# A two-stage gated layer on one core: the gathers of the rank tiles spread over the steps of the first stage, and the sort, the loads and ScalarE's order in the opening rearranged

## What is computed

```python
# layer 1: of 4 contexts the one that the token's id picks serves as gate, up and down weight
hn = layernorm(x)
e = minimum(ids // 6250, 3)
x = x + tanh(g_xattn) * where_e( (silu(hn @ C[e].T) * (hn @ C[e].T)) @ C[e] )
# layer 2: 16 experts, the best 2 of each token, at most 256 tokens to an expert, and a shared one
xt = layernorm(x)
scores = sqrt(softplus(xt @ gate_w.T)); idx = top_2(scores + gate_b)
y = sum over the two of w * W2[e] @ (silu(xt @ W1[e].T) * (xt @ W3[e].T))   + the shared expert
x = x + tanh(g_ffn) * y
```

## Time and profile before

| | us |
|---|---|
| median of 3 runs | 496.58 |
| lowest, highest | 496.21, 497.57 |
| the profiled execution, its own time | 497.83 |
| its span, first to last instruction | 496.0 |

### The profile page before, as it was taken

How to read it: one execution, slowest core, us unless ns; L and a number is a source line. 1 busy time by engine, 2 the same in 40 slices (tenths; PEclk the granted TensorE clock), 3 DMA queues, 4 the chain that set the end, 5 groups by cost and what they waited for, 6 DMA issues and landing times.

```text
span 496.0 us, 7772 instructions
## 1 busy us (share of the span) xinstructions
PE 464.3 (94%) x2496; PEld 393.5 (79%) x2496; DVE 329.9 (67%) x707; ACT 257.8 (52%) x379; POOL 208.2 (42%) x175
## 2 busy tenths in 40 slices
PE   1889999999999939999999999999999999999993
PEld 1358887888888728888888999999999999888982
DVE  5669998998987534358937976666666666666520
ACT  4744544545553333363253576666666666666531
POOL 0612443664334733541636724444427444332242
PEclk9989999999999969999999999999999999999997
DMA  8626545666545713233629999998969988897545
GB/s 320 233 82 234 170 152 168 233 233 223 169 174 199 246 56 113 86 50 48 85 65 230 211 301 313 234 258 255 261 225 264 280 268 247 259 258 223 107 58 70
DMA packets 29164, 95.02 MB, mean 192 GB/s; under 512 B 4816, under 2 KB 5328, under 8 KB 28624
## 3 DMA queue, kind: packets, MB, share of 16 engines
q0 software_dynamic: 17040, 43.66, 35.4%
q1 hardware_dynamic: 11808, 50.98, 30.8%
q10 hardware_dynamic: 288, 0.01, 0.0%
HBM read 67.50 MB, written 28.70 MB: 194 GB/s over the span
## 4 chain that ended last, share of the span: by engine, by line
PE 84%; DVE 7%; issue 3%; DMA 2%; ACT 1%; another core or an unknown queue 1%; POOLq 0%; POOL 0%; DVEq 0%; ACTq 0%
PE psG L1251 46%; PE psY L1251 28%; PE psT L1256 6%; PE psG L1495 1%; DMA front<-in_x,idx 1%; ACT arena L619 1%; DMA tok_i<-in_ids 1%; DVE stats L908 1%; DVE xh_sb L881 1%; DVE gu L897 1%; DVE arena L886 0%; PE psG L1279 0%; DVE stats L915 0%; DVE big L834 0%
## 5 line engine op out<-in xcount | busy, mean ns | idle before, releaser
L1251 PE MATMUL psY<-arena 128*128 (+2 forms) x372 | 94.4, 401 | 0.0
L1251 PEld LDWEIGHTS psY<-arena 128*128 128x128 f32 (+1 forms) x372 | 67.5, 188 | 13.3
L497 POOL DMA_INDIRECT ht<-out,idx x32 | 34.6, 1081 | 78.2 <-PE psT L1256 62.4
L1251 PE MATMUL psY<-slot,arena 128*128 128x512 f32 (+1 forms) x240 | 61.1, 399 | 0.0
L1026 DVE TENSOR_TENSOR slot<-raw,slot 128x1536 fp32r<-128x1536 f32 x25 | 43.9, 1757 | 23.8 <-ACT slot L615 23.1
L1251 PE MATMUL psG<-arena 128*128 x228 | 58.0, 403 | 0.0
L1026 DVE TENSOR_TENSOR arena<-raw,arena 128x1536 fp32r<-128x1536 f32 x24 | 42.1, 1758 | 22.9 <-ACT arena L615 19.5
L1251 PE MATMUL psG<-arena,slot 128*128 128x512 f32 x216 | 52.6, 399 | 0.0
L1251 PEld LDWEIGHTS psY<-slot,arena 128*128 128x128 f32 (+1 forms) x240 | 43.7, 189 | 9.0 <-ACT xh_sb L659 0.3
L1251 PEld LDWEIGHTS psG<-arena 128*128 128x128 f32 x228 | 42.0, 190 | 10.2 <-issue 1.9
L1251 PEld LDWEIGHTS psG<-arena,slot 128*128 128x128 f32 x216 | 41.1, 193 | 8.5
(11 more groups left out here) (221 smaller groups left out, 809.1 us busy)
## 6 DMA issues: line engine op xcount, KB each, us to landing
raw<-in_w SPq DMA_DIRECT2D x51, 768.0 KB
padded<-xh_sb SPq DMA_DIRECT2D x19, 256.0 KB
raw<-in_ctx_t SPq DMA_DIRECT2D x2, 1024.0 KB, 8.9
ht<-in_ctx_t SPq DMA_DIRECT2D x1, 1024.0 KB, 13.3
xh_sb<-in_ctx_t SPq DMA_DIRECT2D x1, 1024.0 KB, 15.4
out<-log_sb SPq DMA_DIRECT2D x4, 256.0 KB
ht<-out,idx POOLq DMA_INDIRECT x32
xb<-in_x,idx POOLq DMA_INDIRECT x19
```

The costliest lines, as they stand in the source:

```text
L497: pool.indirect_dma_start(ht[:, n, :], None, halves_of_out, slots(e * NA + a, 0)).then_inc(g_here[n], 16)
L1251: ins = pe.matmul(ps, left[a], right[b], start=n == 0 and m == 0, stop=n == total - 1 and m == 2)
```

## The change

1. **Rank gathers.** Tiles 4 to 10 are gathered one in each step from 13 to 19, behind the step's scatter; tile 11 after the loop's last scatter, and 12 to 15 behind it. `row_tile` gives tiles 4 to 7 and 12 to 15 `ht`, tiles 8 and 9 `ys`, tiles 10 and 11 `xa`. The waits for free buffers follow.
2. **Sort.** The triangular matrices, `ones` and `iota` are made bf16 by one activation of ACT (`marks`, over `gu`), and the count totals are bf16 (`tot`), so the prefix matmuls are bf16. `hold` is an instruction that counts on `chain` without a wait. Some instructions go without waits, a multiply and a reduction go ahead of the wait for PE. The one-hot blocks are 16 instructions of 128x128 that come last, and each of the 16 matmuls waits for its own. The list's first column is signalled ahead of its second. The table of contexts by tile (`tile_e`) comes after the list.
3. **Loads.** The fourth context, the bias and the zeros are issued once POOL has issued the first gather (`first_out`).
4. **Contexts.** Context 2 goes by PE and context 1 by DVE. ACT's order: `high_ctx(2)` behind two `take_rest(0, ..)`, `take_rest(2, 0)` and `(2, 1)` behind the first norm, `high_ctx(3)` in step -1.

The core of the diff:

```diff
@@ row_tile
-            return ht[:, j % 4, :] if j % 8 < 4 else front[:, j % 4, :]
+            return ht[:, j % 4, :] if j // TB != 2 else (ys, xa)[j % TB // 2][:, j % 2, :]
@@ sync
-            for e in range(E1):
+            for e in range(E1 - 1):
                 sp.dma_start(ctx_raw(e), ctx_t[e, :, :]).then_inc(ctx_here[e], 16)
+            sp.wait_ge(first_out, 1)
+            sp.dma_start(ctx_raw(E1 - 1), ctx_t[E1 - 1, :, :]).then_inc(ctx_here[E1 - 1], 16)
             sp.dma_start(bias_b[:, :], gate_b).then_inc(in_bias, 16)
@@ gpsimd: rank_gather
-                if j >= 8:
+                if j // TB == 2:
+                    pool.wait_ge(h_ready, 4 if j % TB < 2 else NT)
                     pool.wait_ge(bT_ps, j - 7)
-                elif j >= 4:
-                    pool.wait_ge(hT_ps, NT)
+                elif j >= TB:
+                    pool.wait_ge(bT_ps, j - 3 if j < 2 * TB else j - 7)
@@ gpsimd: the loop over t
-                if t == NT - 1:
-                    for j in range(TB, 2 * TB):
-                        rank_gather(j)
-                if t == NT:
-                    for j in range(2 * TB, 3 * TB):
-                        rank_gather(j)
+                if ROWS0 < t <= ROWS0 + 2 * TB - 1:
+                    rank_gather(t - ROWS0 + TB - 1)
+            rank_gather(3 * TB - 1)
@@ scalar
+            act.wait_ge(in_const, 16)
+            act.activation(marks[:, :], cst[:, 0:4 * P], ACT.Copy).then_inc(digits_ready, 1)
...
             high_ctx(0)
             high_ctx(1)
+            take_rest(0, 0)
+            take_rest(0, 1)
             high_ctx(2)
-            take_rest(0, 0)
-            high_ctx(3)
-            for i in range(1, KD):
-                take_rest(0, i)
-            take_rest(1, 0)
-            take_rest(1, 1)
+            take_rest(0, 2)
+            take_rest(0, 3)
@@ scalar: step
+                if known == -1:
+                    high_ctx(3)
                 if known in (-1, 0):
-                    take_rest(1, known + 3)
+                    take_rest(2, known + 3)
...
+                if known == FIRST:
+                    take_rest(2, 0)
+                    take_rest(2, 1)
@@ vector
             for e in range(1, E1):
-                link(dve.tensor_scalar(S(e), S(0), float(VOCAB1 // E1 * e), None, ALU.is_ge))
-            link(dve.tensor_scalar(S(4), S(1), -1.0, 1.0, ALU.mult, ALU.add))
+                hold(dve.tensor_scalar(S(e), S(0), float(VOCAB1 // E1 * e), None, ALU.is_ge))
+            link(dve.tensor_scalar(S(7), S(0), float(VOCAB1 // E1 * (E1 - 1)), None, ALU.is_ge))
+            hold(dve.tensor_scalar(S(4), S(1), -1.0, 1.0, ALU.mult, ALU.add))
+            hold(dve.tensor_tensor(S(15), S(1), S(2), ALU.add))
             link(dve.tensor_tensor(S(5, 2), S(1, 2), S(2, 2), ALU.subtract))
-            link(dve.tensor_copy(S(7), S(3)))
-            link(dve.tensor_tensor(S(3), S(1), S(2), ALU.add))
-            link(dve.tensor_tensor(S(3), S(3), S(7), ALU.add))
...
+            link(dve.tensor_tensor(S(21, E1), run, S(4, E1), ALU.mult))
+            hold(dve.tensor_tensor(S(15), S(15), S(3), ALU.add))
+            link(dve.tensor_reduce(S(16), S(21, E1).rearrange("p (e j) -> p j e", e=E1), AX.X, ALU.add))
             dve.wait_ge(r1_pre, 1)
...
-            dve.tensor_tensor(onehot1, along(digits[:, :], NJ), over(lo_digit[:, :], P), ALU.is_equal)
...
+            for j in range(NJ):
+                dve.tensor_scalar(onehot1[:, j, :], digits, S(12)[:, j:j + 1], None, ALU.is_equal).then_inc(r1_hot, 1)
...
-            low_ctx(2, 0, 1)
+            link(low_ctx(1, 0, 1))
@@ tensor
-            pe.matmul(psY[0][:, 0:E1], tri, S12(small)[:, 1:E1 + 1], start=True, stop=False)
-            pe.matmul(psY[0][:, 0:E1], low_tri, S12(small)[:, 0:E1], start=False, stop=True)
-            pe.matmul(psY[0][:, E1:2 * E1], ones, S12(small)[:, 0:E1], start=True, stop=True).then_inc(r1_pre, 1)
-            pe.wait_ge(r1_hot, 1)
+            pe.matmul(psY[0][:, 0:E1], mark_tri, tot[:, 1:E1 + 1], start=True, stop=False)
+            pe.matmul(psY[0][:, 0:E1], mark_low, tot[:, 0:E1], start=False, stop=True).then_inc(r1_pre, 1)
+            pe.matmul(psT[0][:, 0:E1], mark_ones, tot[:, 0:E1], start=True, stop=True).then_inc(r1_pre, 1)
             for j in range(NJ):
+                pe.wait_ge(r1_hot, j + 2)
```

More of the change, by code:

```diff
@@ L171, in gated_layer @@
         gu = sb("gu", [P, NI * CAP])
+        marks = gu[:, 0:2 * P].bitcast(BF16)
+        mark_tri, mark_low, mark_ones, digits = (marks[:, c:c + P] for c in (C_TRI, C_LOW, C_ONE, C_IOTA))
         xh_sb = sb("xh_sb", [P, 2, 2 * D])
@@ L427, in scatter @@
             def scatter(t):
+                if t == 0:
+                    pool.wait_ge(r1_idx, 2)
                 pool.wait_ge(xh_ready, t + 1)
@@ L549, in take_rest @@
             def take_rest(e, i):
-                act.wait_ge(rest_ps, e * KD + i + 1)
+                act.wait_ge(rest_ps, e // 2 * KD + i + 1)
+                if e and i == KD - 1:
+                    act.wait_ge(ctx_lo_done, 2)
                 o = (e * KD + i) * D
@@ L782, in link, with hold @@
                 dve.wait_ge(chain, links[0])
+            def hold(ins):
+                links[0] += 1
+                ins.then_inc(chain, 1)
             def S(n, w=1):
@@ L823, in _ @@
             link(dve.tensor_tensor_scan(run, ones[:, 0:E1 * NJ], S(4, E1), 0.0, ALU.mult, ALU.add))
-            run = run.rearrange("p (e j) -> p e j", e=E1)
-            dve.tensor_copy(S(12)[:, 1:E1 + 1], run[:, :, NJ - 1]).then_inc(r1_tot, 1)
+            per_e = run.rearrange("p (e j) -> p e j", e=E1)
+            dve.tensor_copy(tot[:, 1:E1 + 1], per_e[:, :, NJ - 1]).then_inc(r1_tot, 1)
+            link(dve.tensor_tensor(S(21, E1), run, S(4, E1), ALU.mult))
+            hold(dve.tensor_tensor(S(15), S(15), S(3), ALU.add))
@@ L826, in _ @@
+            link(dve.tensor_reduce(S(16), S(21, E1).rearrange("p (e j) -> p j e", e=E1), AX.X, ALU.add))
             dve.wait_ge(r1_pre, 1)
-            link(dve.tensor_tensor(S(17, E1).rearrange("p (e j) -> p e j", e=E1), run, over(psY[0][:, 0:E1], NJ), ALU.add))
-            link(dve.tensor_tensor(S(21, E1), S(17, E1), S(4, E1), ALU.mult))
-            link(dve.tensor_reduce(S(25), S(21, E1).rearrange("p (e j) -> p j e", e=E1), AX.X, ALU.add))
+            link(dve.tensor_tensor(S(17, E1).rearrange("p (e j) -> p e j", e=E1),
+                                   S(4, E1).rearrange("p (e j) -> p e j", e=E1), over(psY[0][:, 0:E1], NJ), ALU.mult))
@@ L830, in _ @@
+            link(dve.tensor_reduce(S(25), S(16, E1 + 1).rearrange("p (e j) -> p j e", e=E1 + 1), AX.X, ALU.add))
             link(dve.tensor_scalar(SI(0), S(25), -1.0, None, ALU.add))
-            link(dve.tensor_scalar(SI(1), SI(0), P - 1, None, ALU.bitwise_and))
-            link(dve.tensor_copy(lo_digit[:, :], SI(1)))
-            dve.wait_ge(digits_ready, 1)
-            dve.tensor_tensor(onehot1, along(digits[:, :], NJ), over(lo_digit[:, :], P), ALU.is_equal)
+            hold(dve.tensor_scalar(SI(1), SI(0), P - 1, None, ALU.bitwise_and))
@@ L835, in _ @@
             link(dve.tensor_scalar(SI(2), SI(0), 7, None, ALU.arith_shift_right))
+            hold(dve.tensor_copy(S(12), SI(1)))
             link(dve.tensor_copy(S(26), SI(2)))
-            link(dve.tensor_tensor(S(27), S(26), S(3), ALU.add))
+            link(dve.tensor_tensor(S(27), S(26), S(15), ALU.add))
             q = q_tok[0]
             link(dve.tensor_tensor(q_w[0][:, :, 0:NT], along(iota[:, 0:NT], NJ), over(S(27), NT), ALU.is_equal))
-            dve.tensor_tensor(q[:, :, 0:NT], q_w[0][:, :, 0:NT], over(tok_part[0], NT), ALU.mult)
+            hold(dve.tensor_scalar(q[:, :, 0:NT], q_w[0][:, :, 0:NT], tok_part[0][:, 0:1], None, ALU.mult))
@@ L845, in _ @@
+            link(dve.scalar_tensor_tensor(src, psY[1][:, NT:2 * NT], float(PAD), S(30, 2)[:, 0:NT], ALU.add, ALU.add))
+            dve.tensor_scalar(idx1[:, :, 0], src, float(TOK - 1), None, ALU.min).then_inc(r1_idx, 1)
+            dve.tensor_copy(idx1[:, :, 1], src).then_inc(r1_idx, 1)
+            dve.wait_ge(r1_pre, 2)
+            link(dve.tensor_copy(S(13)[:, 0:E1], psT[0][:, 0:E1]))
             link(dve.tensor_scalar(S(14)[:, 0:E1], S(13)[:, 0:E1], 1.0 / P, -(P - 1.0) / P, ALU.mult, ALU.add))
@@ L950, in step @@
                                 low_h()
+                                dve.wait_ge(ctx_lo_done, 1)
+                                dve.nop(nofuse=True).then_inc(ctx_lo_done, 1)
                     nw(dve.scalar_tensor_tensor(T, T, -10 / 3 * RS_W, T, ALU.add, ALU.mult))
@@ L1284, in _ @@
                 rest(0, i)
-            rest(1, 0)
-            rest(1, 1)
+            rest(2, 0)
+            rest(2, 1)
             pe.wait_ge(rest_taken, KD)
@@ L1324, in step @@
                 if known in (-1, 0):
-                    rest(1, known + 3)
+                    rest(2, known + 3)
                 if ROWS0 <= known < ROWS0 + TB:
@@ L1542 @@
 N_OF = {bc: n for n, bc in enumerate(SEQ)}
```

(2 more changed lines are left out.)

25 lines of the change are left out of this document (9 added, 16 removed).

## The result

The changed kernel takes 490.58 us (490.04 to 491.09) beside 496.44 of the kernel before (496.21 to 497.57) on the same chip: 0.988 times, 95% interval 0.987 to 0.990. The forecast was 481.7. Of 14.9 us foreseen, 5.9 came.

What follows compares the result with a forecast made beforehand. PE was taken to bound the kernel except in the opening, 12 us around 175 and the tail. Savings of 3.9 (opening) and 11.0 (middle) took the median 496.58 down 14.9 to 481.7, range 479.5 to 493.5.

Steps and rivals of the forecast that it cites:

- Counts, places, one-hots, issue: Opening's sort: counts at 5.5, places and weights done at 9.0, one-hots 2.9 long, first gather issued 13.0 instead of 15.70.
- Landing and rests: Opening: first gather lands at 17.0, norm ends 20.9, PE's rests end 21.6, transposes start 21.7 instead of 25.63.
- The cover of the other edits: Opening: moved loads, later fourth context and ACT's new order hidden behind other work, costed at nothing, 1 us kept in range.
- whatever is won moves all that follows: After both open places: PE has work without a hole, so the savings of 3.9 and 11.0 carry to the end.
- The rival "slower": Opening: ACT waits for the late fourth context, delaying step 0; 499.5 if it lands at 31; slower given 0.05.
- The price of the stall: Middle, 173.32 to 188.29: 14.97 us for work that took 4.0 just before, so the stall costs 11.0.
- Its cause: Middle: PE's signals seen 6 and 9 us late, taken to come from POOL's unbroken run of 14 DMAs.
- I take the stall as gone, 11.0 saved: Middle: with POOL's run 10 long and starting later, the whole stall vanishes; stall gone given 0.47.
- the second rival: Middle: the stall shrinks or moves to a later half-up; around 487 us (485 to 490.5), chance 0.16.
- the signs named for a wrong forecast: Changed profile: `gate(1)` again starting us after its matmuls, or ACT idling on the fourth context.
- A smaller term: Middle: tile 11's gather, issued at 169.6, lands by 173.0, before PE wants it at 173.9, so costs nothing.
- the likeliest case: Whole kernel: stall gone and opening's gain kept, 481.7 us (480.3 to 484), chance 0.47.

Runs made afterwards that it cites:

- loads_later: Changed kernel with fourth context and bias issued behind the third gather, zeros behind first weights, fourth context's high part behind second norm: 488.45 us, 0.985 times before, chip 12.
- logits_later: Changed kernel with the first block's four logits sends held until the second block's logits are ready: 493.80 us, 0.995 times the kernel before, chip 12.
- gap_fourth: Changed kernel with the first four logits sends held until the third up group, on chip 12: 487.14 us, 0.981 times the kernel before.
- the two traces of chip 10: Kernel before and changed kernel, both unchanged, on chip 10: 483.14 and 485.74 us, ratios 1.001 and 1.004 to the kernel before.
- rank_again: Kernel before with the rank gathers' new places and buffers alone, on chip 10: 484.10 us, 1.002 times the kernel before.
- before_again: Kernel before, unchanged, profiled on chip 10: 483.14 us beside 483.30, ratio 1.001.

## Why the prediction was right and wrong

- **Counts, places, one-hots, issue:** right, each a little early (issue 12.44 for 13.0). The pitch of the one-hots was 2.69 / 16 = 0.17 for 0.18. (The lower end of the opening's range is a little too high: with one-hots of 6.1 its own terms leave about 1.5, not 2. Nothing hung on it.) The Trainium skill's terms ("VectorE: DVE Perf Modes", "Side-by-side: where the cycles go for N=2048 bf16"), with a start-up paid each time, would have given an estimated 3.2 to 4.8 for the 16; the trace doesn't agree for instructions that follow each other unheld.
- **Landing and rests:** right. Tile 0 had its statistics at 16.35 (17.0) and its transposes at 21.05 (21.7).
- **"The cover of the other edits": this step failed.** "I cost these at nothing, and keep 1 us": the gathers of tiles 1 to 5 beside 2 MB of loads. They cost 3.8, the 4.6 won at the transposes less the 0.8 left at the second product. Tile 2's, "wanted 3 to 4 us after tile 0 is", took 8.88 from issue against the 6.03 of the earlier trace rows, and held tile 0's own low part through DVE's order. The opening's 3.9 shrank to 0.8 at the second product (33.81 against 34.63), and to 0.1 by 107 us, so that "whatever is won moves all that follows" didn't hold in stage 1 either. The rival "slower" had the right place and the wrong victim: ACT took up the fourth context at 22.23 without a wait for it; the gathers that shared the engines with it were late. loads_later shows 5 us there.
- **The price of the stall:** right: 11.0 by the earlier trace rows, 11.3 by the chip without it.
- **Its cause:** right as far as it went. The hold follows POOL's run (logits_later, gap_fourth) and not the DMA share. What in the run does it isn't shown.
- **"I take the stall as gone, 11.0 saved": this step failed.** A run of ten was still long enough: of 11.3 us 4.5 stayed. That was the second rival, with 0.16; its range ended at 490.5. Neither of the signs named for a wrong forecast showed: `gate(1)` was in time and ACT didn't idle on the fourth context, but `gate(2)` started 2.9 us after its matmuls. The trace of before had runs of up to 7 without harm and one of 14 with it, and nothing to choose between for 10.
- **A smaller term:** tile 11 "lands by 173.0", but PE waited for it until 174.21, 0.56 us.
- **What no row of one trace could tell:** that the hold belongs to some chips. On the others the change is 0.4 to 0.6% slower.

The measured 490.58 lies inside the stated 479.5 to 493.5, 6.6 above the likeliest case; it got there by two losses at once, each of which the sum had at nothing, and no case described both. So the sum 3.9 + 11.0 became, by the two traces, 0.1 + 6.3, against 5.9 by the medians. (11.3 less the 4.5 that stayed is 6.8; the moved gathers take back 0.5 in the middle, as the two traces of chip 10 show, 2.6 apart ahead of it and 3.1 behind it.)

## What to carry to other kernels

When loads are moved behind a first gather, price every transfer that is issued with them, and read which engine's order stands behind its landing; here one late tile held back another that had long been there. When a hole has releasers that the profile can't name, compare the end of the producer with the start of the consumer, and look at what another engine issues in between; break up its row of DMA issues by a rest, holding back those that aren't urgent, and look that they don't make a new row elsewhere. And profile the kernel before on every chip that an experiment falls on: a gain may be the repair of something that only some chips have.

## What the runs showed of the hardware

- On chip 12 and the first chip, where before takes 496 us, PE's signals reach DVE and ACT 3 to 10 us late when POOL has issued indirect DMAs without a break for more than 7 us. The last of them come about 2 us after the run's end (run to 180.58, seen at 182.56; run to 198.35, seen at 200.10), others while it still goes on (175.56 and 180.47). It was so with 14 DMAs, ten, and twelve sends of logits; after six it wasn't, and with eight it was under 2 us. On chips 4, 6 and 10 it wasn't seen with any run. Why the chips differ is open.
- After PE idles of 4.3 to 5.4 us in the opening the granted clock was at half speed (1.2 of 2.4 GHz) for 3.4 to 6.8 us, after 2.12 (before) and 2.29 us (rank_again) for 3.4; after 0.63 us (loads_later) and 1.80 us (before on chip 10) it stayed at full speed, and so it did after one of 2.47 in loads_later, at 179. So the length of the idle alone doesn't decide it here.
- On chip 12 and the first chip smaller losses come in stage 1 between 58 and 107 us, 1.0 us in the kernel before and 1.3 after, against the same kernels on chip 10. Most of it comes at one place, and there too a signal of PE is late, by 1.3 us, though POOL has issued only two DMAs (73.06 and 74.33) after a pause of 2.98. The timeline of before:

```profile
73.06 0.95 POOL L420 DMA_INDIRECT front<-in_x,idx  x1 [2.98 <-ACT front L567]
...
73.23 0.63 PE L1256 MATMUL psT<-cst,gu 128*128 128x128 f32 x4
...
75.16 0.60 ACT L573 ACTIVATE arena<-psT 128x512 fp32r<-128x512 f32 x1 [1.66 <-PE psT L1256]
```

and of before_again:

```profile
71.03 0.63 PE L1256 MATMUL psT<-cst,gu 128*128 128x128 f32 x4
...
71.70 0.60 ACT L573 ACTIVATE arena<-psT 128x512 fp32r<-128x512 f32 x1 [0.41 <-PE psT L1256]
```

The four transposes end at 73.86 and 71.66, and ACT starts 1.30 and 0.04 us behind them. So short delays of PE's signals come without a long run of POOL; what makes them is open.
